# Row loads in two halves between the maxima transfers, and normalised tiles one per step, in a four-stage attention and mixture-of-experts kernel

## The chip, the cores and the metric

The kernel runs on one core of a Trainium2 chip. The metric is the device time of one execution in microseconds (us). Engines are named as in the profile: PE (TensorE matmul) and PEld (its weight loads), DVE (VectorE), ACT (ScalarE), POOL (GpSimd) and SP (SyncE, which here only issues transfers). SPq is SP's queue of instructions.

## What is computed

The input x is (4, 512, 256) in float32, the context has the same shape. Four stages follow each other, each adding to x: an attention without projections and with rotated queries and keys and a linear position bias (16 heads of 16), a top-1 expert layer, an attention with projections, and a top-k expert layer. The change touches the two attention stages alone.

```python
    x = x + _L0_xattn_ref(_layernorm(x, axis=-1), ctx_1024, ctx_1024, 16)
    x = x + _L0_ffn_ref(_layernorm(x, axis=-1), ...)
    x = x + _L1_xattn_ref(_layernorm(x, axis=-1), ctx_1024, ctx_1024, ...)
    x = x + _L1_ffn_ref(_layernorm(x, axis=-1), ...)
...
        scores = jnp.einsum('bqhd,bkhd->bhqk', q, k) * scale + bias[None]
        attn = jax.nn.softmax(scores, axis=-1)
        out = jnp.einsum('bhqk,bkhd->bqhd', attn, v)
```

## The kernel before, in words

One function, `attention`, makes both attention stages; `layer` is 0 or 1. The work is cut into 16 slots: slot s is batch b = s // 4 and group g = s % 4 of four heads. A slot takes four steps, one for each chunk of 128 keys, so step t belongs to slot t // 4 and a batch takes 16 steps. The program of each engine is written out as a loop over steps from -8 to 75.

For every half step PE makes a score tile with keys on the partitions (L596, `scores`), a second score tile with queries on the partitions for the row maxima of eight steps later (L581, `maxima_scores`, AHEAD = 8), and the weighted sum with the values (L615, `weigh`). The two score tiles share a ring of three units in PSUM: a new maxima tile takes the unit of the score tile whose exponentials ACT has just written (L719), and a new score tile the unit of the maxima tile that DVE has just reduced (L786). So PE waits for ACT one half step back.

The way of the maxima is: DVE reduces 8 tiles of slot s (L786), negates them (L792, L793), PE transposes them in step 4s-4 (L479, job "m"), ACT copies them to `max_t` (L655), and SP sends them into four more rows of `qa` (L364, `load_max(s)`, two transfers of 16 KB). PE needs them in step 4s, at the first score tile of slot s, which waits for `max_in`. m2, m6 and m10 stand below for `load_max` of slots 2, 6 and 10.

The rows of queries and keys of a batch come from two DRAM scratch tensors. `load(b, part)` fetches them: part 0 is groups 0 and 1 of the batch, part 1 is groups 2 and 3 (batch 0 is cut otherwise and is loaded ahead of the steps). Each part is four transfers of 384 KB (`rows_in_place`, L327): query rows and key rows, each for two partition halves; in layer 1 the key rows of batch 1 are loaded early, so that its parts have two transfers. Before the change both parts of a batch stand behind each other in SP's program, ahead of the maxima transfer of step 16b-12, which is m2, m6 and m10 for batches 1, 2 and 3. The maxima tiles need part 0 in step 16b-8 and part 1 in step 16b.

POOL rotates and splits the keys and queries of later batches and stores them in the scratch tensors: three transfers of 512 KB for the keys of a batch (L254), three of 256 KB for each pair i of query tiles (L259). Pair i is the half i % 2 of batch i // 2; there are eight.

For each pair ACT normalises two tiles of 128 x 256 (L687, `normed(i)`), two instructions behind each other at the start of step `q_at[i] - 3`; PE transposes them in step `q_at[i]` (L496), and ACT copies the result out (L664 in layer 0). In layer 0 `q_at` is 6 and 10 for pairs 4 and 5 and 22 and 26 for pairs 6 and 7, in layer 1 it is 2, 6, 18 and 22. In front of the exponentials the order is therefore: pair 4 in step 3, pair 5 in step 7 behind the copy of pair 4 in step 6, pair 6 in step 19, pair 7 in step 23 behind the copy of pair 6 in step 22. The first four pairs are normalised before the first exponential.

At the end of a slot (step 4s+4) ACT copies the slot's sums out of PSUM (L725, `a_out_sb`); two such copies in steady state lie one slot apart.

Of the kernel before, what the change touches and what calls it, by code (L numbers as in the profile page):

```python
# [6 lines left out]
ACT = mybir.ActivationFunctionType  # L7
# [8 lines left out]
B, T, D = 4, 512, 256  # L16
H, HD = 16, 16
# [6 lines left out]
NG = H // HG  # L24
# [119 lines left out]
def attention(nc, m, layer, dram):  # L144
# [8 lines left out]
    with ExitStack() as ctx:  # L153
# [77 lines left out]
        x = m.x  # L231
# [16 lines left out]
        def groups(b, part):  # L248
            cut = 1 if b == 0 else 2
            return (0, cut) if part == 0 else (cut, NG)  # L250
# [54 lines left out]
        with nc.Block() as block:  # L305

            @block.sync
            def _(sp):
# [26 lines left out]
                def load(b, part):  # L335

                    if part == 0:
                        if b == 0:
                            if layer == 0:
                                sp.wait_ge(k_first, 48)  # L340
                            sp.wait_ge(q_first, 96)
                        else:
                            if layer == 0:
                                sp.wait_ge(k_stored, 48 * b)
                            for j in range(2):
                                sp.wait_ge(q_stored[j], 48 * b)
                        if b >= 2:
                            sp.wait_ge(st_full, 8 * NG * (b - 1))
                    if layer == 1 and b >= 2:
                        load_keys(b, part)  # L350
                    for par in range(2):
                        rows_in_place(qa, q_scr, b, part, par).then_inc(loaded[part], 16)
                        if layer == 0:
                            rows_in_place(ka, k_scr, b, part, par).then_inc(loaded[part], 16)
# [40 lines left out]
                for t in steps:  # L395
                    for b in range(1, B):
                        if layer == 0 and b >= 2 and t == 16 * b - 38:
                            load_ctx(b)
                        for part in range(2):
                            if t == (2 if b == 1 else 16 * b - 14) + 2 * part:  # L400
                                load(b, part)
                    for job in ended.get((t, 1), []):
                        if job[0] == "m":
                            load_max(job[1])

            @block.gpsimd
            def _(pool):
# [238 lines left out]
            def _(act):  # L646
# [26 lines left out]
                            act.wait_ge(misc_full, index["a", b - 1, 1] + 1)  # L673
                        nc.scalar.copy(att_t[:, c], misc[:]).then_inc(misc_free, 1)

                def normed(i):

                    act.wait_ge(stats_done, (1 if i < 2 else 2) if layer == 0 else min(i // 2 + 1, 3))
                    if i >= 2:
                        act.wait_ge(misc_full, index[norm_kind, i - 2] + 1)  # L680
                    for j in range(2):
                        k = 2 * i + j
                        to, of = xn[:, i % 2, j], x[:, k]
                        if layer == 0:
                            to = to.rearrange("p (d e h) -> p h e d", e=2, d=HD)
                            of = of.rearrange("p (h e d) -> p h e d", e=2, d=HD)
                        nc.scalar.activation(to, of, ACT.Identity, bias=neg_mean[:, k:k + 1], scale=rstd[:, k:k + 1]).then_inc(xn_ready, 1)  # L687

                def values(n):

# [9 lines left out]
                        values(n)  # L700
                for job in first:
                    if job == (norm_kind, 0):
                        normed(0)
                        normed(1)
                    act_job(job)
                if layer == 1:
                    for n in range(4, 2 * B):
                        values(n)
                for t in steps:
                    for i in range(2, 2 * B):  # L710
                        if t == max(q_at[i] - 3, steps[0]):
                            normed(i)
                    for half in range(2):
                        n = 2 * t + half
                        if 0 <= t < STEPS:
# [1022 lines left out]
```

## Time and profile before

| what | value |
|---|---|
| device time, median of 3 runs (lowest, highest) | 1086.34 us (1085.20, 1089.04) |
| the profiled execution's own time | 1078.34 us |
| its span, first to last instruction | 1076.5 us |
| mean granted TensorE clock | 0.953 |
| PE busy | 944.4 us, 88% of the span |
| DVE, ACT, POOL busy | 605.6, 513.6, 300.5 us |
| layer 0's attention, about | first exponential at 75.2 us, last slot copied out near 265 us |
| layer 1's attention, about | first exponential at 565.2 us, end near 800 us |

The profiled execution lies 1.8 us above its span, and 8.0 us under the median of the timed runs. A PE that is busy 88% of the time still has gaps, and what they wait for is read from the timeline. Idle time of another engine costs only where PE waits for it.

### The profile page before, as it was taken

The numbers are of one execution on the slowest core, as the hardware profiler recorded it, in microseconds if no ns is written. First come the engines' busy times: TensorE is split into PE (matmuls) and PEld (weight loads), VectorE is DVE, ScalarE is ACT, GpSimd is POOL, SyncE is SP. The second block draws the span as 40 slices with busy tenths as digits, with TensorE's granted clock in tenths as the row PEclk, the third lists the DMA queues.
The fourth block names the chain that finished last, engine by engine and source line by source line (L and its number), as shares of the span: only waits on it lengthen the run. The fifth ranks groups of instructions, "written<-read, shape, count | busy, mean of one in ns | idle before, by whom it ended". The sixth has DMA issues, their size and how long they took to land. (4 is left out here: it accounts for less than half of the span.)

```text
span 1076.5 us, 17358 instructions
## 1 busy us (share of the span) xinstructions
PE 944.4 (88%) x6842; PEld 650.2 (60%) x6842; DVE 605.6 (56%) x1011; ACT 513.6 (48%) x777; POOL 300.5 (28%) x280
## 2 busy tenths in 40 slices
PE   0159999899798999999779999999979999999993
PEld 0023334343576999999653444444449999999993
DVE  7678979794432111110586766979314836655553
ACT  1027777678423322332326775767633035445550
POOL 5467843000001222221132122000000245554222
PEclk9999999899869999999997999999987999999997
DMA  9978372500439999996884061320006224555316
GB/s 159 234 206 200 94 195 58 96 4 4 153 134 373 325 338 345 339 345 220 186 202 91 33 119 62 73 51 4 4 2 236 79 59 133 141 169 146 98 21 175
DMA packets 52148, 158.96 MB, mean 148 GB/s; under 512 B 7792, under 2 KB 27888, under 8 KB 41392
## 3 DMA queue, kind: packets, MB, share of 16 engines
q1 hardware_dynamic: 35952, 121.96, 38.7%
q0 software_dynamic: 12912, 29.63, 11.3%
q10 hardware_dynamic: 3216, 6.43, 1.6%
q8 instruction: 47, 0.77, 0.3%
q14 instruction: 21, 0.17, 0.1%
HBM read 116.18 MB, written 40.76 MB: 146 GB/s over the span
## 5 line engine op out<-in xcount | busy, mean ns | idle before, releaser
L786 DVE TENSOR_REDUCE a_row_max<-ps_ring 128x2 f32<-128x1024 f32 x256 | 308.9, 1222 | 79.0 <-PE ps_ring L581 76.6
L719 ACT ACTIVATE a_probs<-ps_ring 128x1024 f32<-128x1024 f32 x256 | 260.7, 1022 | 102.1 <-PE ps_ring L596 100.2
L615 PE MATMUL ps_out<-a_probs,a_vaug 128*32 128x256 f32 x2048 | 166.7, 399 | 2.5 <-ACT a_out_sb L725 1.5
L581 PE MATMUL ps_ring<-a_ka,a_qa 52*128 52x512 f32 (+1 forms) x512 | 120.1, 473 | 54.4 <-DMA a_ka<-scratch_k_scr 44.2
L596 PE MATMUL ps_ring<-a_qa,a_ka 56*128 56x512 f32 (+1 forms) x512 | 131.7, 511 | 5.7 <-DMA a_qa<-a_max_t 3.7
L1056 ACT ACTIVATE e_hid<-ps_ring,e_wts 128x128 f32<-128x128 f32 x184 | 52.3, 368 | 120.2 <-PE ps_ring L1156 86.2
L596 PEld LDWEIGHTS ps_ring<-a_qa,a_ka 56*128 56x128 f32 (+1 forms) x512 | 49.1, 188 | 98.6 <-issue 67.3
L581 PEld LDWEIGHTS ps_ring<-a_ka,a_qa 52*128 52x128 f32 (+1 forms) x512 | 51.5, 199 | 86.9 <-issue 38.9
L1445 ACT ACTIVATE e_hr<-ps_ring 128x512 fp32r<-128x512 f32 x64 | 38.3, 598 | 118.9 <-PE ps_ring L1516 118.9
L1516 PE MATMUL ps_ring<-e_xt,e_wr 128*128 128x512 f32 x384 | 88.7, 390 | 0.4 <-DVE e_xt L1584 0.4
L615 PEld LDWEIGHTS ps_out<-a_probs,a_vaug 128*32 128x32 f32 x2048 | 41.1, 109 | 78.4 <-issue 72.2
L1156 PEld LDWEIGHTS ps_ring<-e_xst,e_wts 128*128 128x128 f32 x736 | 87.1, 195 | 1.9 <-issue 0.8
L1156 PE MATMUL ps_ring<-e_xst,e_wts 128*128 128x128 f32 x736 | 87.4, 278 | 0.6 <-DVE e_xst L1255 0.6
L1168 PE MATMUL ps_ring<-e_wts,e_hid 128*128 128x256 f32 x368 | 83.5, 380 | 0.3 <-ACT e_hid L1056 0.3
L1516 PEld LDWEIGHTS ps_ring<-e_xt,e_wr 128*128 128x128 f32 x384 | 71.6, 188 | 15.0 <-issue 0.6
L1604 DVE TENSOR_TENSOR e_hr<-e_hf,e_hr 128x512 fp32r<-128x512 f32 x64 | 44.4, 694 | 54.4 <-ACT e_hf L1448 54.4
L1168 PEld LDWEIGHTS ps_ring<-e_wts,e_hid 128*128 128x128 f32 x368 | 68.3, 191 | 8.8 <-ACT e_hid L1056 0.5
L1409 POOL DMA_INDIRECT scratch_acc<-e_ys,e_token x32 | 56.9, 1779 | 54.8 <-DVE e_ys L1598 50.9
L997 POOL DMA_INDIRECT scratch_ys<-e_ys,e_to_row x23 | 22.8, 993 | 121.6 <-DVE e_ys L1264 121.6
L1400 POOL DMA_INDIRECT e_xg<-scratch_xl,e_token x32 | 32.2, 1008 | 76.4 <-PE ps_ring L1500 47.9
L1264 DVE TENSOR_TENSOR e_ys<-ps_ring,e_wts 128x256 f32<-128x256 f32 x23 | 9.8, 425 | 74.9 <-PE ps_ring L1168 74.9
L1261 DVE TENSOR_TENSOR e_xst<-ps_misc,e_rms_t 128x256 f32<-128x256 f32 x22 | 9.3, 425 | 75.4 <-PE ps_misc L1137 75.4
(229 smaller groups left out, 1275.0 us busy)
## 6 DMA issues: line engine op xcount, KB each, us to landing
e_wts<-in_w SPq DMA_DIRECT2D x23, 1156.0 KB, 8.2
e_wts<-in_w SPq DMA_DIRECT2D x23, 1024.0 KB, 7.7
e_wf<-in_w SPq DMA_DIRECT2D x16, 1024.0 KB, 5.3
scratch_q_scr<-a_qst POOLq DMA_DIRECT2D x36, 256.0 KB, 3.2
a_qa<-scratch_q_scr SPq DMA_DIRECT2D x24, 384.0 KB, 10.2
a_ka<-scratch_k_scr SPq DMA_DIRECT2D x24, 384.0 KB, 12.2
scratch_k_scr<-a_kst POOLq DMA_DIRECT2D x9, 512.0 KB, 15.8
scratch_xl<-e_xn SPq DMA_DIRECT2D x8, 512.0 KB, 5.0
```

What stands on the lines that cost most here:

```text
L581: ins = pe.matmul(to[:, par], qa[rows, b % 2, g, p, qt * P:(qt + 1) * P], ka[rows, b % 2, g, p], start=True, stop=True)
L596: ins = pe.matmul(to[:, par], ka[rows, b % 2, g, p, kc * P:(kc + 1) * P], qa[rows, b % 2, g, p], start=True, stop=True)
L615: ins = pe.matmul(m.ps_out[VW * h:VW * (h + 1), cols], vaug[:, b % NV, kc, HG * g + h], probs[:, t % 3, h, cols], start=(kc == 0 and half ...
L719: nc.scalar.activation(probs[:, t % 3, 2 * half:2 * half + 2], unit("s", n), ACT.Exp, scale=HD ** -0.5).then_inc(exp_done, 1)
L786: dve.tensor_reduce(row_max[:, s % 3, qt, :, p], unit("m", n), AX.X, ALU.max).then_inc(mx_read, 1)
L1056: nc.scalar.activation(hid[:, k, fc], m.ps_st[:, 2 * k + half, q * P:(q + 1) * P], ACT.Silu, bias=wts[:, k, w1_cols + FC * D + fc:w1_cols ...
L1156: ins = pe.matmul(m.ps_st[:, 2 * k + half, q * P:(q + 1) * P], wts[:, k, c * F + fc * P:c * F + (fc + 1) * P], xst[:, k, c], start=(c == 0 ...
L1168: ins = pe.matmul(m.ps_max[:, k, 0:D], hid[:, k, fc], wts[:, k, w1_cols + fc * D:w1_cols + (fc + 1) * D], start=(fc == 0), stop=(fc == FC ...
L1409: pool.indirect_dma_start(dram["acc"], bass.IndirectOffsetOnAxis(token[:, e, b:b + 1], 0), ys[:, e % 2, b], None, compute_op=ALU.add).then ...
L1445: nc.scalar.activation(hr[:, 0, fc], m.ps_st[:, fc % 4], ACT.Gelu_apprx_tanh)
L1516: ins = pe.matmul(m.ps_st[:, fc % 4], wr[:, k, wp, c * F + fc * P:c * F + (fc + 1) * P], xt[:, xp, c], start=(c == 0 and (wp, xp) == (0, 0 ...
L1604: dve.tensor_tensor(hr[:, 1, fc], hf[:, fc % 4], hr[:, 0, fc].bitcast(F32), ALU.subtract).then_inc(h_split, 1)
```

## The change

In SP's program `load(b, part)` moves behind the maxima transfer of the same step, and its step becomes `16 * b - 15 + 4 * part` for every batch: part 0 in step 16b-15, behind the maxima transfer of step 16b-16, and part 1 in step 16b-11, behind that of step 16b-12. So one maxima transfer (m2, m6, m10) now stands between the two parts. Part 1 of batches 2 and 3 gets a wait of its own, for the first maxima tile of the batch before's group 2 (`mx_full`).

In ACT's program `normed(i)` becomes `normed(i, j)`, one tile each, in steps `q_at[i] - 4` and `q_at[i] - 3`. The first four pairs, which are normalised ahead of the exponentials, keep their order, and so does the loading of batch 0.

```diff
@@ load(b, part), SP @@
                         if b >= 2:
                             sp.wait_ge(st_full, 8 * NG * (b - 1))
+                    elif b >= 2:
+                        sp.wait_ge(mx_full, 8 * (NG * (b - 1) + groups(b, part)[0]) + 1)
@@ loop over steps, SP @@
-                        for part in range(2):
-                            if t == (2 if b == 1 else 16 * b - 14) + 2 * part:
-                                load(b, part)
                     for job in ended.get((t, 1), []):
                         if job[0] == "m":
                             load_max(job[1])
+                    for b in range(1, B):
+                        for part in range(2):
+                            if t == 16 * b - 15 + 4 * part:
+                                load(b, part)
@@ normed, ACT @@
-                def normed(i):
+                def normed(i, j):
...
-                    for j in range(2):
-                        k = 2 * i + j
...
-                        if t == max(q_at[i] - 3, steps[0]):
-                            normed(i)
+                        for j in range(2):
+                            if t == max(q_at[i] - 4 + j, steps[0]):
+                                normed(i, j)
```

SP's queue in layer 0 around the load of batch 3, before the change: the maxima transfer of slot 9 (L364), eight row loads (L327), then the maxima transfer of slot 10. Names in brackets are semaphores.

```order
L364 DMA a_qa<-a_max_t 4x2x512 [waits a0_st_full,a0_misc_free]
L364 DMA a_qa<-a_max_t 4x2x512
L327 DMA a_qa<-scratch_q_scr 48x2048 [waits a0_q_stored1,a0_st_full,a0_q_stored0,a0_k_stored]
L327 DMA a_ka<-scratch_k_scr 48x2048
L327 DMA a_qa<-scratch_q_scr 48x2048
L327 DMA a_ka<-scratch_k_scr 48x2048
L327 DMA a_qa<-scratch_q_scr 48x2048
L327 DMA a_ka<-scratch_k_scr 48x2048
L327 DMA a_qa<-scratch_q_scr 48x2048
L327 DMA a_ka<-scratch_k_scr 48x2048
L364 DMA a_qa<-a_max_t 4x2x512 [waits a0_st_full,a0_misc_free]
L364 DMA a_qa<-a_max_t 4x2x512
```

The same place of SP's queue after the change (line numbers are those of the changed file, where L366 is L364 of before):

```order
L327 DMA a_qa<-scratch_q_scr 48x2048 [waits a0_q_stored1,a0_st_full,a0_q_stored0,a0_k_stored]
L327 DMA a_ka<-scratch_k_scr 48x2048
L327 DMA a_qa<-scratch_q_scr 48x2048
L327 DMA a_ka<-scratch_k_scr 48x2048
L366 DMA a_qa<-a_max_t 4x2x512 [waits a0_st_full,a0_misc_free]
L366 DMA a_qa<-a_max_t 4x2x512
L327 DMA a_qa<-scratch_q_scr 48x2048 [waits a0_mx_full]
L327 DMA a_ka<-scratch_k_scr 48x2048
L327 DMA a_qa<-scratch_q_scr 48x2048
L327 DMA a_ka<-scratch_k_scr 48x2048
L366 DMA a_qa<-a_max_t 4x2x512 [waits a0_st_full,a0_misc_free]
L366 DMA a_qa<-a_max_t 4x2x512
```

The first maxima transfer in this piece is slot 10's: it had eight row loads ahead of it and now has four, and slot 11's, the last one here, now has four loads ahead of it where it had none.

ACT's queue in layer 0 in steps 4 to 8, before the change: the copy of slot 0's sums, the maxima copy of slot 2, four exponentials (steps 5 and 6), the copy of pair 4, both tiles of pair 5, four exponentials (steps 7 and 8) and the next copy of sums.

```order
L725 COPY a_out_sb<-ps_out 128x512
L655 CAST a_max_t<-ps_misc 8x512
L719 ACTIVATE a_probs<-ps_ring 128x1024 x4
L664 COPY a_qx<-ps_misc 128x512
L687 ACTIVATE a_xn<-x_res,a_neg_mean,a_rstd 128x8x2x16 x2
L719 ACTIVATE a_probs<-ps_ring 128x1024 x4
```

The same piece after the change:

```order
L729 COPY a_out_sb<-ps_out 128x512 [waits a0_pv_done]
L658 CAST a_max_t<-ps_misc 8x512 [waits a0_max_in0,a0_misc_full]
L723 ACTIVATE a_probs<-ps_ring 128x1024 [waits a0_pv_done,a0_st_full] x2
L689 ACTIVATE a_xn<-x_res,a_neg_mean,a_rstd 128x8x2x16 [waits a0_misc_full,a0_stats_done]
L723 ACTIVATE a_probs<-ps_ring 128x1024 [waits a0_pv_done,a0_st_full] x2
L667 COPY a_qx<-ps_misc 128x512 [waits a0_q_ready,a0_misc_full]
L689 ACTIVATE a_xn<-x_res,a_neg_mean,a_rstd 128x8x2x16 [waits a0_misc_full,a0_stats_done]
L723 ACTIVATE a_probs<-ps_ring 128x1024 [waits a0_pv_done,a0_st_full] x4
```

One of the two tiles went from step 7 to the start of step 6, ahead of that step's two exponentials; the copy of pair 4 and the other tile stayed.

## Rows read from the trace of the kernel before

**Rows 1.** The page: busy time of PE over the whole span.

```profile
PE 944.4 (88%) x6842; PEld 650.2 (60%) x6842; DVE 605.6 (56%) x1011; ACT 513.6 (48%) x777; POOL 300.5 (28%) x280
```

**Rows 2.** Waits: who waited for L364, whole span (us, times); PE's wait, 75 to 265 us.

```profile
  PE ps_ring L596: 3.7, 2
...
PE ps_ring L581 <- ACT a_probs L719: 3.6, 4, 1.2
```

**Rows 3.** Timeline of SP's queue in layer 0: start, length, line, transfer, count.

```profile
91.92 1.35 SPq L364 DMA_DIRECT2D a_qa<-a_max_t  x2
...
143.61 1.35 SPq L364 DMA_DIRECT2D a_qa<-a_max_t  x2
...
183.96 0.32 SPq L327 DMA_DIRECT2D a_qa<-scratch_q_scr  x1
...
194.06 1.35 SPq L364 DMA_DIRECT2D a_qa<-a_max_t  x2
```

**Rows 4.** One transfer at a time: issue and time from issue to landing, us.

```profile
L327 SPq DMA_DIRECT2D a_ka<-scratch_k_scr x1: 422/422/422, 185.3 to 185.3; - x1
DMA to landing us min/median/max: 10.5/10.5/10.5
...
L327 SPq DMA_DIRECT2D a_ka<-scratch_k_scr x1: 423/423/423, 187.3 to 187.3; - x1
DMA to landing us min/median/max: 17.6/17.6/17.6
...
L254 POOL DMA_DIRECT2D scratch_k_scr<-a_kst x2: 731/731/731, 90.2 to 91.0; - x2
DMA to landing us min/median/max: 13.0/13.7/14.5
```

**Rows 5.** Timeline of PE, layer 0; in brackets idle time ahead and its releaser.

```profile
99.97 0.50 PE L581 MATMUL ps_ring<-a_ka,a_qa 52*128 52x512 f32 x2 [1.16 <-ACT a_probs L719]
100.39 0.64 PE L615 MATMUL ps_out<-a_probs,a_vaug 128*32 128x256 f32 x8
...
102.05 0.50 PE L596 MATMUL ps_ring<-a_qa,a_ka 56*128 56x512 f32 x2 [0.43 <-DMA a_qa<-a_max_t]
...
103.28 0.49 PE L596 MATMUL ps_ring<-a_qa,a_ka 56*128 56x512 f32 x2
...
138.14 0.50 PE L581 MATMUL ps_ring<-a_ka,a_qa 52*128 52x512 f32 x2 [0.65 <-ACT a_probs L719]
...
151.67 0.50 PE L581 MATMUL ps_ring<-a_ka,a_qa 52*128 52x512 f32 x2 [1.17 <-ACT a_probs L719]
152.09 1.07 PE L615 MATMUL ps_out<-a_probs,a_vaug 128*32 128x256 f32 x8
...
155.97 0.50 PE L596 MATMUL ps_ring<-a_qa,a_ka 56*128 56x512 f32 x2
...
205.12 0.80 PE L596 MATMUL ps_ring<-a_qa,a_ka 56*128 56x512 f32 x2 [3.23 <-DMA a_qa<-a_max_t]
```

**Rows 6.** Stretch 152 to 154 us: busy time of each engine, PEclk, DMA share, GB/s.

```profile
152.00:154.00 2.00, 2.00 (x14) 0.91 (x12) 1.64 (x3) 0.52 (x1) 1.86 (x4) 0.54 0.33 80
```

**Rows 7.** Timeline of ACT, layer 0: the copies at the ends of three slots.

```profile
181.35 0.59 ACT L725 COPY a_out_sb<-ps_out 128x512 f32<-128x512 f32 x1
...
192.99 0.58 ACT L725 COPY a_out_sb<-ps_out 128x512 f32<-128x512 f32 x1
...
221.60 0.59 ACT L725 COPY a_out_sb<-ps_out 128x512 f32<-128x512 f32 x1
```

**Rows 8.** Timeline of ACT in step 19 of layer 0: pair 6, then two exponentials.

```profile
135.83 1.41 ACT L687 ACTIVATE a_xn<-x_res,a_neg_mean,a_rstd 128x256 f32<-128x256 f32 x2
137.04 1.95 ACT L719 ACTIVATE a_probs<-ps_ring 128x1024 f32<-128x1024 f32 x2
```

**Rows 9.** Waits of PE in layer 1, 560 to 660 us: us, times, longest.

```profile
PE ps_ring L581 <- ACT a_probs L719: 0.6, 2, 0.4
```

**Rows 10.** Timeline of DVE and POOL, layer 0: the negations beside POOL's work.

```profile
101.77 0.24 DVE L792 TENSOR_SCALAR a_neg_max<-a_row_max 128x16 fp32r<-128x16 f32 x1
...
126.17 1.29 DVE L792 TENSOR_SCALAR a_neg_max<-a_row_max 128x16 fp32r<-128x16 f32 x1
...
126.14 1.28 POOL L282 TENSOR_TENSOR a_kf<-a_kf 128x512 f32<-128x512 f32 x1
```

More of the change, by code:

```diff
@@ L680, in normed @@
                         act.wait_ge(misc_full, index[norm_kind, i - 2] + 1)
-                    for j in range(2):
-                        k = 2 * i + j
[L683 to L687, printed above, removed]
+                    k = 2 * i + j
+                    to, of = xn[:, i % 2, j], x[:, k]
+                    if layer == 0:
+                        to = to.rearrange("p (d e h) -> p h e d", e=2, d=HD)
+                        of = of.rearrange("p (h e d) -> p h e d", e=2, d=HD)
+                    nc.scalar.activation(to, of, ACT.Identity, bias=neg_mean[:, k:k + 1], scale=rstd[:, k:k + 1]).then_inc(xn_ready, 1)
                 def values(n):
@@ L702, in _ @@
                     if job == (norm_kind, 0):
-                        normed(0)
-                        normed(1)
+                        for i in range(2):
+                            for j in range(2):
+                                normed(i, j)
                     act_job(job)
@@ L710, in _ @@
                     for i in range(2, 2 * B):
-                        if t == max(q_at[i] - 3, steps[0]):
-                            normed(i)
+                        for j in range(2):
+                            if t == max(q_at[i] - 4 + j, steps[0]):
+                                normed(i, j)
                     for half in range(2):
```

## Prediction

> **What bounds the kernel now.** I began with the page: PE is busy for 944.4 us, 88% of the span [rows 1], so a change that takes no work from PE can only win what PE loses in gaps, and what PE loses by running at the lower clock behind a gap. The next view was who waits for the two things that the change touches. For the maxima transfers (L364) PE's matmuls wait 3.7 us in two places, and for the exponentials in layer 0 they wait 3.6 us in four places [rows 2]. Then the timelines of PE, SP and ACT, to see what is ahead of each wait.
>
> The two waits for maxima are the first score tile of slot 2, at 102.05 us with 0.43 us of idle time, and that of slot 10, at 205.12 us with 3.23 us [rows 5]. Slot 10's transfers were issued at 194.06 us, 10 us after the row loads of batch 3 began at 183.96 us [rows 3]. The last row load, issued at 187.3 us, landed 17.6 us later, at 204.9 us; the fourth of the eight, issued at 185.3 us, landed after 10.5 us, at 195.8 us [rows 4]. PE goes on 0.2 us after the last of the eight has landed. The maxima are small and are served behind 3 MB of rows: I read it as a queue in order, and the landing times grow evenly along it.
>
> What it costs is more than the wait. Slots end at 181.35 and 192.99 us, 11.64 us apart; the next two take 28.61 us together, to 221.60 us [rows 7], against 23.28 us. So batch 3's stall costs **5.3 us**: 3.2 us of wait, and 2.1 us in which the matmuls behind it take 0.80 us in place of 0.50 us [rows 5].
>
> At batch 2 there is little wait for maxima, but a low clock: from 152 to 154 us the granted clock is 0.54 [rows 6], nearly the lower level of 1.2 GHz. From the weighted sum at 152.09 us to the score tile at 155.97 us it is 3.88 us; the same row of work at batch 1 takes 2.89 us, from 100.39 to 103.28 us, of which 0.43 us is the wait [rows 5]. So 3.88 - 2.46 = **1.4 us** is lost. What PE did before the clock fell was to stand still for 1.17 us at 151.67 us [rows 5], for ACT.
>
> That is the second kind of gap. ACT normalises two tiles in 137.04 - 135.83 = 1.21 us ahead of the exponentials of a step [rows 8], and PE's next maxima tile waits for the first of these: 0.65 us at 138.14 us, and 1.16 and 1.17 us where the copy of the pair before also stands ahead (99.97 and 151.67 us) [rows 5]. The fourth of the four, pair 4's, is what is left of 3.6 us, about 0.6 us [rows 2].
>
> **The change, part by part.**
>
> *Loads in halves.* No transfer is added or dropped. m2, m6 and m10 have four loads ahead of them in place of eight. By the landing times of batch 3 the fourth has landed at 195.8 us [rows 4], so m10, issued at 194.06 us [rows 3], should be in place near 196 to 197 us, 5 us before PE asks at about 201.9 us. At batches 1 and 2 POOL's key stores share the engines, but half of 20 us of loads still leaves m2 and m6, issued at 91.92 and 143.61 us [rows 3], several us in hand. So the waits go: 0.4 us at batch 1, and 5.3 us at batch 3, its low clock included. For batch 2 the bounds are 0 (the clock falls all the same) and 1.4 us; I take 1.4 us, since the gap that stands ahead of the fall shrinks as well, next paragraph.
>
> What is queued behind: SP waits for nothing new in fact. The new wait of part 1 (batches 2 and 3) is for a maxima tile of step 16b-16, and the transfer ahead of it in SP's queue belongs to step 16b-12, which is later. Behind part 1 stands the maxima transfer of the next slot (m3, m7, m11). It comes a slot, 11.6 us, after part 1, and four loads take 195.8 - 184.0 = 11.8 us, so it lands about 1 us late at most, and PE wants it four steps after its issue. Part 1's rows are wanted in step 16b and are issued in step 16b-12 or so, three slots, 35 us, ahead. Cost nothing; without that cover a late part 1 would stop PE for as long as it is late.
>
> *Tiles one per step.* The same instructions, each 0.605 us of ACT. A step without other work has hidden 1.21 - 0.65 = 0.56 us of the pair, so a single tile costs it 0.05 us. For pairs 4 and 6: 0.65 becomes 2 x 0.05, saved 0.55 us each. For pairs 5 and 7 the step behind the copy goes from 1.165 us to 1.165 - 0.605 = 0.56 us, and the step before pays 0.05 us: saved 0.5 us each. Together **2.1 us**. Bounds: 0 if the step that takes the tile over has no room, 3.6 us if all four gaps close. I take the middle by the slack read at 138.14 us.
>
> *Layer 1.* No wait of PE for maxima is left for it: the two of layer 0 make up 0.43 + 3.23 of the 3.7 us in the whole span [rows 2, 5]. Its waits for exponentials around the pairs are 0.6 us in two places [rows 9]; I take 0.2 us, bounds 0 and 0.6 us. The loads' halves win nothing there.
>
> *DVE beside POOL.* One row speaks for a loss. The negation at 126.17 us took 1.29 us beside a POOL tensor operation from 126.14 us that took 1.28 us; at 101.77 us it took 0.24 us [rows 10]. The order on POOL and DVE is unchanged, but the slots with a copy of queries get half a microsecond shorter, so a negation can start half a microsecond earlier against POOL's work. From the row: at worst one POOL operation of 1.3 us more is waited for, in each of two slots. The slot of 101.77 us is one of the two, and there the negation was hardly held, so I take the row that is nearest: cost 0, bounds 0 and 2.6 us. The Trainium skill (SBUF — State Buffer, section "SBUF: two separate sides") says that DVE and GpSimd share a pair of ports as a lock, which one holds for a whole instruction while the other is fully blocked. By that rule, the trace agrees (1.29 against 0.24 us), and it is the one rule there that speaks for a loss; by it in full the sum below would be 2.6 us less.
>
> **Sum.** 0.4 + 1.4 + 5.3 + 2.1 + 0.2 = **9.4 us** of 1078.34 us, the profiled execution's own time, so 1068.9 us for an execution like it. The median of the runs shown lies 8.0 us above that execution; I carry the gain over unchanged: 1086.3 - 9.4 = **1076.9 us**. Low end of the gain: 0.4 + 0 + 5.3 + 0 + 0 - 2.6 = 3.1 us; high end: 0.4 + 1.4 + 5.3 + 3.6 + 0.6 = 11.3 us.
>
> **Rivals.** A measurement of this kernel tells no change from one of about 0.3%, 3.3 us.
>
> *The halves of the tiles win nothing (faster still).* PE is fully busy in the steps that take the tile over, so each tile moves its delay along. For it: ACT's slack there is only half a microsecond. Against: the two kinds of gap, 0.65 and 1.16 us, differ by just about the copy, as a slack used up once would have it. Gain 9.4 - 2.1 = 7.3 us, 1079.0 us.
>
> *The maxima are not served in the queue's order (no change).* Part 1 is issued right behind m10 and could get ahead of it, as m10 fills only eight partitions. Then m10 lands with the last of the rows as before. For it: one cannot see the maxima's own landing in the trace. Against: in all places PE goes on just when the rows ahead have landed, with nothing behind them to compare. Gain only 2.1 + 0.2 = 2.3 us, 1084.0 us.
>
> *The key stores hold the maxima (slower).* At batches 1 and 2 POOL stores 1.5 MB of keys while the loads run. If m2's completion had to wait for them, it would come when the third store lands, issued at 91.0 us and 14.5 us on its way, at 105.4 us [rows 4], while PE would now ask for it at 101.6 - 1.1 = 100.5 us: a wait of 4.9 us, and the like at batch 2, 9.8 us together, against 5.3 + 2.3 = 7.6 us won elsewhere. That is 2.2 us slower, 1088.5 us, and more with a fall of the clock behind each wait. It decides from 3.8 us per wait on. Against it: before the change PE went on at 102.05 us [rows 5], 3.4 us before that store had landed. The Trainium skill (DMA: Bandwidth & Descriptors, section "Queues, rings and completion order") has a rule of this kind: a transfer's semaphore increment lands only after every earlier write of its DMA engine, across queues. By that rule the stores could hold m2; the trace bears it out only weakly, as the 3.4 us show. The same section says that each engine consumes one queue's descriptors in order and takes turns between queues, with which the 0.2 us at slot 10 agrees.
>
> **How the numbers follow.** Chances: the forecast 0.80, tiles win nothing 0.07, maxima not in order 0.08, key stores 0.05. Faster 0.87, within 0.3% 0.08, slower 0.05. The predicted time is the forecast's, 1076.9 us. Its own range is 1086.3 - 11.3 to 1086.3 - 3.1, 1075.0 to 1083.2 us; the timed runs of before spread by about 2 us to either side, and the stretches of low clock need not fall in the timed runs as they did in this profile, so I widen to 1071.5 to 1083.5 us, which leaves out the no-change and the slower case.
>
> **What would show it.** In layer 0: no PE wait for `a_max_t` at slots 2, 6 and 10; all slots of batch 2 and later without a query pair at 11.6 us, that of slot 9 among them (16.6 us before); granted clock 1.0 from 150 to 260 us; PE's waits for exponentials down from 3.6 to about 1.4 us; eight single tiles of 0.6 to 0.7 us on ACT; loads in two groups 12 us apart, m3, m7 and m11 without a wait. In layer 1 the same length within 0.5 us. I am wrong if PE still waits at slot 10, if m7 or m11 becomes a wait, or if slots without a stall grow by a DVE negation of over 1 us.

## The result, and the profile after

In the first comparison, four executions of each kernel, the changed kernel took **1068.88 us** (1067.97 to 1072.19) and the kernel before 1087.69 us (1085.20 to 1089.82). The ratio is **0.983**, 95% interval 0.980 to 0.987: by the medians 18.8 us faster, where 9.4 us was forecast. 1068.88 us lies under the low end of the range. Of every kernel below, executions more than 1.5% longer than its shortest are left out of the ratios (one of e1, three each of e5 and e16, two of e10), but not out of the medians and ranges. The profiled execution of the changed kernel took 1068.09 us against 1078.34 us before, 10.25 us less.

Its page, busy times over the whole span, answers to [rows 1]: PE's work is the same number of instructions, 4.8 us shorter.

```profile
PE 939.6 (88%) x6842; PEld 645.7 (61%) x6842; DVE 605.4 (57%) x1011; ACT 514.1 (48%) x777; POOL 300.1 (28%) x280
```

PE's waits in layer 0's attention, 60 to 260 us (us, times, longest), answer to [rows 2]: no row for `a_max_t` is left, and the wait for the exponentials fell from 3.6 us in four places to 1.2 us in two.

```profile
PE ps_ring L584 <- ACT a_probs L723: 1.2, 2, 0.6
```

SP's queue around the load of batch 3, and the landing of each half's last row load, answer to [rows 3, 4]. Columns as there.

```profile
182.16 0.42 SPq L327 DMA_DIRECT2D a_ka<-scratch_k_scr  x1
190.98 1.35 SPq L366 DMA_DIRECT2D a_qa<-a_max_t  x2
192.37 0.44 SPq L327 DMA_DIRECT2D a_qa<-scratch_q_scr  x1
...
202.64 1.35 SPq L366 DMA_DIRECT2D a_qa<-a_max_t  x2
```

```profile
L327 SPq DMA_DIRECT2D a_ka<-scratch_k_scr x1: 422/422/422, 182.2 to 182.2; - x1
...
DMA to landing us min/median/max: 11.0/11.0/11.0
...
L327 SPq DMA_DIRECT2D a_ka<-scratch_k_scr x2: 422/422/422, 192.9 to 193.8; - x2
...
DMA to landing us min/median/max: 6.9/8.9/10.8
```

Part 0's last load landed at 182.2 + 11.0 = 193.2 us, 2.2 us behind the issue of m10 and 5.5 us ahead of the score tile that needs it, at 198.75 us, which has no idle time ahead of it. Part 1's last row load lands only at 193.8 + 10.8 = 204.6 us, so m10 was in place before the rows issued behind it, 5.8 us at the least. PE, the timeline at the two places where pairs 5 and 7 stand, and at slots 2 and 10 (it answers to [rows 5]):

```profile
99.74 0.49 PE L584 MATMUL ps_ring<-a_ka,a_qa 52*128 52x512 f32 x2 [0.59 <-ACT a_probs L723]
...
101.32 0.50 PE L599 MATMUL ps_ring<-a_qa,a_ka 56*128 56x512 f32 x2
...
149.89 0.50 PE L584 MATMUL ps_ring<-a_ka,a_qa 52*128 52x512 f32 x2 [0.58 <-ACT a_probs L723]
...
198.75 0.50 PE L599 MATMUL ps_ring<-a_qa,a_ka 56*128 56x512 f32 x2
```

The window of [rows 6] now has PEclk 1.00, and the copies of sums at the ends of slots 8, 9 and 10 (ACT's timeline, answering to [rows 7]) are 11.66 and 11.65 us apart, where batch 3's stall was:

```profile
152.00:154.00 2.00, 2.00 (x22) 0.69 (x20) 1.97 (x4) 1.77 (x2) 1.86 (x3) 1.00 0.88 131
```

```profile
189.90 0.59 ACT L729 COPY a_out_sb<-ps_out 128x512 f32<-128x512 f32 x1
...
201.56 0.59 ACT L729 COPY a_out_sb<-ps_out 128x512 f32<-128x512 f32 x1
...
213.21 0.59 ACT L729 COPY a_out_sb<-ps_out 128x512 f32<-128x512 f32 x1
```

Pair 6 is now two tiles, one in each of two steps (ACT's timeline; [rows 8] shows the pair in one row):

```profile
132.49 0.82 ACT L689 ACTIVATE a_xn<-x_res,a_neg_mean,a_rstd 128x256 f32<-128x256 f32 x1
...
135.10 0.82 ACT L689 ACTIVATE a_xn<-x_res,a_neg_mean,a_rstd 128x256 f32<-128x256 f32 x1
```

**The slots of layer 0.** The distance between two copies of sums is a slot. This table is the ruler for all runs below; the slots not in it agree within 0.1 us in the full kernels (slot 0 aside, see the end) but for slot 2 of e2, 12.93 against 12.33 us; in e5 and e16 slots 2 and 6 are up to 0.8 us longer. The traces of e5 and e16 are of long executions, 298.05 us and 299.27 us, where the medians are 296.31 and 295.81 us. The first two rows are the profiles of before and after, and `e...` are the runs of the next section.

```
us                        slot 1  slot 4  slot 5  slot 9  slot 10
before                     13.97   13.78   14.91   16.64   11.97
after                      13.05   13.17   13.06   11.66   11.65
e3  before, again          14.47   13.76   13.80   15.41   12.29
e4  changed, again         13.28   13.19   13.04   11.63   11.65
e1  loads in halves alone  13.51   13.78   13.52   11.64   11.64
e2  tiles alone            16.10   13.21   13.37   16.55   11.92
e8  before, m10 on POOL    16.28   13.78   14.59   16.36   12.21
e5  stage of before        13.74   13.75   17.36   18.09   12.40
e16 stage of before, again 16.07   13.77   17.00   17.59   12.40
```

### The profile page after: what moved, and what is told of

Its sections match the earlier page's. It is cut to its first block and busy times, and to the rows that moved or that the text cites. A ratio compares the mean times of both kernels' runs of the same rounds, so it can differ in the third digit from the quotient of the medians.

```text
span 1066.3 us, 17370 instructions
## 1 busy us (share of the span) xinstructions
PE 939.6 (88%) x6842; PEld 645.7 (61%) x6842; DVE 605.4 (57%) x1011; ACT 514.1 (48%) x777; POOL 300.1 (28%) x280
## 6 DMA issues: line engine op xcount, KB each, us to landing
scratch_k_scr<-a_kst POOLq DMA_DIRECT2D x9, 512.0 KB, 12.5
```

## The experiments

**The two kernels again, and each part alone** (e1 to e4, one chip, shared with 29 executions of the kernel before, median 1085.57 us, 1079.24 to 1093.26). e3 and e4 have no edit. e1 is the SP part of the diff alone, e2 the ACT part alone:

```diff
@@ e1: loop over steps, SP; ACT as before @@
+                    for b in range(1, B):
+                        for part in range(2):
+                            if t == 16 * b - 15 + 4 * part:
+                                load(b, part)
@@ e2: loop over steps, ACT; SP as before @@
-                        if t == max(q_at[i] - 3, steps[0]):
-                            normed(i)
+                        for j in range(2):
+                            if t == max(q_at[i] - 4 + j, steps[0]):
+                                normed(i, j)
```

> The loads' half of the change alone: row loads in two halves behind maxima transfers, both normalised tiles of a pair in one step as before. The two profiles at hand give the whole change 10.2 us, the timed runs about 18 us. Theory A (the timed executions of the kernel before lose more at the maxima waits and at the low clock behind them than its one profiled execution did): this part alone gives 14 to 17 us of the timed gain. Theory B (the tiles' half of the change is worth more in timed runs than in the profile): it gives 7 us or less. Theory C (the runs shown were drawn from different stages of luck, and the change is worth the 10 us of the profiles): 6 to 8 us. In its trace PE waits for no maxima transfer and still waits about 3.6 us for exponentials in layer 0.

> The tiles' half alone: normalised tiles one per step, row loads as before. By the prediction's sum 2.1 us of gain by the tiles, and up to 1.4 us more if the fall of the clock at batch 2 came from the 1.17 us gap. Theory A: 1 to 4 us. Theory B: 8 to 12 us. Theory C: 2 to 3 us. In its trace the maxima waits at slots 2 and 10 stay or grow, since PE asks earlier, and the waits for exponentials fall from 3.6 to about 1.4 us.

> The kernel before, unchanged, for a second trace and for how far one execution of it lies from another. Theory A: its trace is 5 to 10 us longer than the first one, and the difference lies in layer 0 at slots 2, 6 and 10, with more low clock there. Theory C: the difference lies in other stages or there is none. Timed, no difference: within 0.3%.

> The changed kernel, unchanged, beside the other three on the same chip. Theory A: 15 to 19 us faster than before, and equal to the sum of the two halves within 3 us. Theory C: 9 to 12 us faster. Trace within 2 us of the first one of the changed kernel.

Measured, 12 executions each of e1 to e3 and 6 of e4: **e1 1077.12 us, ratio 0.993** (0.990 to 0.996); **e2 1086.01 us, ratio 1.000** (0.997 to 1.002); **e3 1082.61 us, 0.998** (0.994 to 1.001); **e4 1072.79 us, 0.989** (0.985 to 0.993). By the ratios the loads alone gain 7.5 us, the tiles alone 0.3 us and both together 11.9 us; the intervals are too wide (4.1 to 10.9 us for e1, 7.2 to 16.7 us for e4) to say from the times that the parts don't add up. The traces say it: behind slot 0, layer 0's attention is 5.8 to 7.2 us shorter in e1 than in the two traces of before, 0.6 to 2.0 us longer in e2, and 7.1 to 8.5 us shorter in the changed kernel. The waits of e2, PE in layer 0, show where the tiles' gain went:

```profile
PE ps_ring L596 <- DMA a_qa<-a_max_t: 6.1, 3, 3.8
...
PE ps_ring L581 <- ACT a_probs L720: 1.2, 2, 0.6
```

```profile
103.88 0.50 PE L596 MATMUL ps_ring<-a_qa,a_ka 56*128 56x512 f32 x2 [2.09 <-DMA a_qa<-a_max_t]
```

The exponentials' wait fell by 2.4 us, as in the changed kernel, and the maxima's grew by as much, 3.7 to 6.1 us: PE comes earlier to a transfer that lands when the rows have landed. At slot 2 the wait grew by more than the tiles can give, from 0.43 to 2.09 us, so part of it is this execution's own. In e1 the other half shows: no wait for maxima, and the one for exponentials as it was.

```profile
PE ps_ring L584 <- ACT a_probs L722: 3.7, 4, 1.2
```

e1 also tells against a reason of mine. The gap of 1.17 us that stood ahead of the low clock in batch 2 [rows 5] is still there in e1, but the granted clock stays 1.0. First e1's row of PE, then the window in which [rows 6] have 0.54, in two pieces:

```profile
150.93 0.51 PE L584 MATMUL ps_ring<-a_ka,a_qa 52*128 52x512 f32 x2 [1.17 <-ACT a_probs L722]
```

```profile
152.00:153.00 1.00, 1.00 (x8) 0.65 (x8) 0.93 (x2) 0.00 (x0) 0.94 (x2) 1.00 1.02 139
153.00:154.00 1.00, 1.00 (x14) 0.34 (x10) 0.96 (x4) 0.94 (x1) 0.92 (x2) 1.00 0.96 147
```

And e3, the kernel before itself, holds 1.0 there too:

```profile
144.00:158.00 14.00, 12.63 (x112) 5.15 (x109) 11.02 (x13) 10.95 (x14) 6.54 (x8) 1.00 0.70 188
```

So the 1.4 us of batch 2 belonged to some executions and not to every one.

**The stages apart.** e5 and e6 keep layer 0's attention of the kernel before and of the changed one and leave the three later stages out; e7 keeps the three later stages of the kernel before and leaves the first out. e9 is e5 with the loads in halves (on another chip than e5 to e7).

```diff
@@ the end of the program, e5, e6, e9; e7 has stages[1:] behind a load of x @@
-        for stage in stages:
-            stage()
+        stages[0]()
```

> Layer 0's attention of the kernel before, alone: the other three stages are left out, and x is stored behind it. From the traces at hand: 273.9 to 274.4 us to the last copy of sums, so about 285 us in all. Theory A (the timed executions lose more at the maxima waits than the traces show): its runs spread by 5 us or more, and lie 12 us or more above those of the changed layer alone. Theory C (the stage is worth what the traces show, and the rest of the timed difference comes from the clock in the other stages): spread under 3 us, and 7 to 9 us above the changed one.

> Layer 0's attention with the change, alone: the other three stages are left out. Theory A: 12 us or more below the same stage of before. Theory C: 7 to 9 us below it, as in the traces (191.7 to 193.2 us against 199.1 to 199.5 us from the first exponential on).

> The three stages behind the first attention, alone (of the kernel before; the first attention is left out, so x goes straight into the top-1 experts and the routing differs): how far executions of the rest lie apart. Theory C: spread of 8 to 12 us between its runs, going with the mean granted clock, and most of the spread of the whole kernel. Theory A: under 5 us.

> Layer 0's attention alone (the other three stages left out), with the loads in halves and both tiles of a pair in one step. The same stage took 296.3 us before and 284.7 us with the whole change. If the loads carry the stage's gain: 285.5 to 288 us, runs within 3 us of each other, no wait for maxima; the tiles are then worth 1 to 3 us behind the halves. If the tiles matter more through the clock: 289 us or more.

Measured: e5 296.31 us (291.59 to 299.87, 6 executions), **e6 284.67 us** (283.49 to 285.52, 5), e9 286.76 us (285.71 to 288.07, 5), e7 802.27 us (799.39 to 804.90, 4). The difference e5 - e6 is 11.6 us by the medians of all executions; by the three of e5 that count in the ratio it is 294.20 - 284.67 = 9.5 us. By the same measure the halves alone are worth 294.20 - 286.76 = 7.4 us, where the prediction's terms for them are 7.1 us. The tiles are worth 286.76 - 284.67 = **2.1 us** behind the halves, the forecast's number. More telling is the spread: 8.3 us among six executions of the old stage, 2.0 us among five of the new one. e5's PE timeline at slots 6 and 10: the first was no wait in [rows 5], the second is longer, and the matmuls take 0.8 us behind both:

```profile
158.20 0.80 PE L596 MATMUL ps_ring<-a_qa,a_ka 56*128 56x512 f32 x2 [2.05 <-DMA a_qa<-a_max_t]
...
212.59 0.79 PE L596 MATMUL ps_ring<-a_qa,a_ka 56*128 56x512 f32 x2 [4.67 <-DMA a_qa<-a_max_t]
```

**The maxima on another queue** (e8: the kernel before, but slot 10's two maxima transfers are issued by POOL, with a semaphore of their own; all eight row loads stay ahead of them in time, on SP's queue).

```diff
@@ loop over steps, POOL @@
+                    if layer == 0 and t == 36:
+                        s = 10
...
+                            pool.dma_start(qa[rows, s // NG % 2, s % NG].bitcast(F32),
```

> The kernel before, whole bursts of eight row loads, but the two maxima transfers of slot 10 in layer 0 issued by POOL's queue and counted by a semaphore of their own. If the order within SP's queue is what holds them, as predicted: no wait of PE for maxima at slot 10, slots 9 and 10 at 11.7 us each, layer 0 shorter by 4 to 5 us. If the 16 DMA engines are simply full (a rival not in the prediction): PE waits at slot 10 as before, 3 us or more. The waits at slots 2 and 6 stay.

One execution, 1073.61 us. POOL issued the maxima at 199.04 us, 7.2 us behind the last row load; PE went on only at 209.54 us. POOL's timeline, then SP's last row load and its landing, then PE's timeline:

```profile
199.04 1.18 POOL L464 DMA_DIRECT2D a_qa<-a_max_t  x2 [2.12 <-ACT a_max_t L672]
```

```profile
L336 SPq DMA_DIRECT2D a_ka<-scratch_k_scr x1: 422/422/422, 191.8 to 191.8; - x1
...
DMA to landing us min/median/max: 17.5/17.5/17.5
```

```profile
209.54 0.79 PE L613 MATMUL ps_ring<-a_qa,a_ka 56*128 56x512 f32 x2 [2.95 <-DMA a_qa<-a_max_t]
```

The last rows landed at 191.8 + 17.5 = 209.3 us, and PE went on 0.2 us later, just as in [rows 4, 5]. So place in SP's queue is not what holds the maxima: on a queue of its own a 16 KB transfer is still complete only when 3 MB of earlier rows are. Slots 9 and 10 take 28.57 us together, before 28.61 us.

The DMA view shows when the packets themselves moved (queue, number of packets, MB, share of 16 engines; q1 is SP's queue, q0 POOL's). First e8 from 199.0 to 206.8 us, then from 206.8 to 209.0 us:

```profile
q1 hardware_dynamic: 218, 1.35, 101.2%
```

```profile
q1 hardware_dynamic: 31, 0.12, 33.1%
q0 software_dynamic: 64, 0.03, 10.7%
```

POOL's two transfers were issued at 199.04 us, and for 7.8 us not one of their 64 packets moved, while 218 of the rows' did. The same shows between other transfers, and in both directions. Before the change, POOL's key stores, issued from 89.5 us on behind row loads, moved nothing up to 97.0 us; in the changed kernel, SP's m2, issued at 92.12 us behind the key stores, moved nothing from 92.1 to 94.0 us:

```profile
q1 hardware_dynamic: 218, 1.35, 103.7%
```

```profile
q0 software_dynamic: 210, 0.76, 101.9%
```

With no rows ahead, POOL's queue is not slow: of its stores issued from 104.4 us on, before the change, the first packets moved before 105.5 us.

The Trainium skill (DMA: Bandwidth & Descriptors, section "Queues, rings and completion order") says that a transfer's semaphore increment lands only after every earlier write of its DMA engine, across queues. e8's times agree with that, 209.54 against 209.3 us, but do not test it, since the packets themselves moved late. The turns between queues of which the same section speaks don't show in these rows, 218 packets to none.

**Both halves behind the maxima** (e10, the new stage alone, the other three left out) and **the tiles a step earlier** (e11 in the stage alone, e12 in the full changed kernel):

```diff
@@ e10, SP @@
-                            if t == 16 * b - 15 + 4 * part:
+                            if t == 16 * b - 11:
@@ e11, e12, ACT @@
-                            if t == max(q_at[i] - 4 + j, steps[0]):
+                            if t == max(q_at[i] - 5 + j, steps[0]):
```

> Layer 0's attention alone, with the tiles one per step, but both parts of a batch behind each other again, one slot later than before: behind the maxima transfers of slots 2, 6 and 10 and ahead of those of slots 3, 7 and 11. If the length of the whole burst (20.6 us from the first issue to the last landing) against a slot is what stops PE: the waits for maxima move to slots 3, 7 and 11, 2 to 4 us each, and the stage takes 293 to 298 us. If the place of the burst was the matter: no such wait, and 284 to 287 us. A small wait for the rows of part 0 is possible in either case, since they are wanted four steps after their issue.

> Layer 0's attention alone, changed stage, with the two tiles of a pair another step earlier (steps q_at - 5 and q_at - 4), so that no tile stands behind the copy of the pair before. If the gaps of 0.6 us left in steps 7 and 23 come from copy and tile together: they go, the two slots with a pair and a copy take 12.5 us in place of 13.06, the stage 1 us less (283.5 us). If ACT's slack is used up in those steps anyway: no change.

> The whole changed kernel with the tiles another step earlier, as in e11, in both attention layers. If the gaps go: 1 us under the changed kernel, that is 1070 to 1073 us and 11 to 15 us under before; not to be told from it by timing alone, so the slots in the trace decide. A loss in layer 1 would show as a slot longer than 15.2 or 21.7 us.

e10 took **306.25 us** (302.94 to 309.74), about 21 us more than e6, and by neither theory: m3, m7 and m11 were no wait, but PE now waited for the rows of part 0 themselves. Its waits and the first place:

```profile
PE ps_ring L584 <- DMA a_ka<-scratch_k_scr: 15.2, 3, 5.4
```

```profile
109.94 0.79 PE L584 MATMUL ps_ring<-a_ka,a_qa 52*128 52x512 f32 x2 [5.35 <-DMA a_ka<-scratch_k_scr]
```

The eight loads were issued from 96.48 us on, PE wanted part 0 8.1 us later and had it after 13.5 us. So part 0 can't be issued three steps ahead of its need; the changed kernel's seven are enough. The experiment did not test what I meant it for, whether a burst of eight holds the next maxima.

e11 took 283.48 us (282.24 to 285.63), 1.2 us less than e6 with the ranges overlapping, on another chip; e12 **1070.89 us, ratio 0.990** (0.986 to 0.993), no better than the changed kernel. The 0.6 us gaps do not close, they move to the step with the copy of sums (e12, PE's timeline), and in layer 1 slots 3 and 4 grew by 0.46 and 0.49 us:

```profile
93.83 0.49 PE L584 MATMUL ps_ring<-a_ka,a_qa 52*128 52x512 f32 x2 [0.58 <-ACT a_probs L723]
...
143.88 0.51 PE L584 MATMUL ps_ring<-a_ka,a_qa 52*128 52x512 f32 x2 [0.61 <-ACT a_probs L723]
```

**Where the rest of 18.8 us is** (e13 to e16, another chip, shared with 11 executions of the kernel before, median 1082.45 us, 1077.95 to 1093.95). e13 is the changed kernel without an edit, e14 is e7 again, e15 the same cut of the changed kernel (layer 0's attention left out), e16 is e5 again.

> The changed kernel a third time, with more runs of both. If the true gain is what the stages show (7 to 9.5 us in layer 0, 0.6 us in layer 1): 8 to 12 us, ratio 0.989 to 0.9925. If the first comparison (18.8 us, four runs each) showed something real beyond the stages: 15 us or more.

> The three stages behind the first attention, alone, of the kernel before, a second time: 799 to 805 us as the first time.

> The same three stages of the changed kernel (layer 0's attention left out): from the traces of layer 1, 0.6 us less than before. If the timed gain beyond the stage of layer 0 is real and comes from the other stages: 3 us or more less. If not: within 2 us.

> Layer 0's attention of before, alone, a second time (other three stages left out). If its ordinary executions lose more at the maxima than the first trace did: median of the undisturbed runs 294 us or more. If they lose the same: 292 to 294 us, that is 7.5 to 9.5 us above the changed stage. In the trace: waits at slots 2, 6 and 10 of 3.5 to 7 us in all.

Measured: **e13 1075.34 us, ratio 0.988** (0.982 to 0.994); e14 810.61 us (805.25 to 811.71); e15 806.06 us (801.93 to 808.21), with ratios to the kernel before of 0.7475 (0.7443 to 0.7507) and 0.7434 (0.7399 to 0.7469); e16 295.81 us (290.94 to 299.77). e16's trace, slots 1, 5 and 9, and each window's PEclk (third number from the end) at 0.84 to 0.86:

```profile
92.89:108.96 16.07, 14.11 (x109) 5.50 (x108) 11.32 (x13) 10.78 (x15) 9.73 (x13) 0.85 0.87 218
...
147.49:164.49 17.00, 14.13 (x110) 5.45 (x109) 11.34 (x13) 10.75 (x14) 8.92 (x11) 0.84 0.74 196
...
200.69:218.28 17.59, 13.43 (x106) 5.11 (x105) 11.27 (x13) 9.13 (x10) 0.72 (x1) 0.86 0.66 106
```

The stages of the whole kernels, from the traces (us). An attention runs from its first exponential to its last copy of sums, and the expert layers are what lies behind each; "behind slot 0" is layer 0's attention from the first copy of sums on. The last column is the whole execution:

```
                        layer 0  behind slot 0  first experts  layer 1  last experts  execution
before                   199.13         183.53         290.87   225.03        286.25    1078.34
e3  before, again        199.51         182.15         290.51   222.86        291.34    1080.41
e8  before, m10 on POOL  202.66         185.52         289.96   221.09        281.74    1073.61
e2  tiles alone          199.09         184.16         291.43   224.21        290.53    1083.42
e1  loads alone          191.86         176.37         291.93   224.76        284.79    1070.20
after                    191.68         175.04         294.95   222.07        283.22    1068.09
e4  changed, again       193.20         175.09         291.87   222.84        287.52    1071.24
e13 changed, third       189.94         174.93         297.48   223.98        288.22    1076.94
```

The expert layers are untouched by the change, and the last one alone takes 281.74 to 291.34 us. Its windows before, in e3 and after (PEclk 0.93, 0.92, 0.94), and the first expert layer's in e13:

```profile
790.25:1076.50 286.25, 260.94 (x1740) 240.93 (x1740) 157.72 (x304) 106.29 (x157) 98.51 (x67) 0.93 0.42 118
```

```profile
787.26:1078.60 291.34, 264.48 (x1740) 244.19 (x1740) 157.73 (x304) 106.41 (x157) 98.54 (x67) 0.92 0.41 116
```

```profile
783.08:1066.30 283.22, 257.52 (x1740) 237.40 (x1740) 157.67 (x304) 106.39 (x157) 98.49 (x67) 0.94 0.42 120
```

```profile
265.42:562.90 297.48, 271.18 (x1668) 236.17 (x1668) 86.69 (x266) 90.23 (x255) 61.64 (x63) 0.91 0.81 268
```

This answers what e3 was run for. Its execution is 2.1 us longer than the first profile of the same kernel, and layer 0 is not the reason: behind slot 0 it is 1.4 us shorter, while the last expert layer is 5.1 us longer. e8 has the longest layer 0 of the eight, and yet the shortest execution of the four that keep the eight row loads together (before, e3, e8, e2). e14 missed its forecast of 799 to 805 us: the same kernel took 802.27 us on e7's chip and 810.61 us on e14's.

By their ratios (1 less the ratio, times the time before) the three comparisons of the same two kernels gave 18.2, 11.9 and 12.9 us. The first is of four executions each, with an interval of 14.6 to 21.6 us; the later ones, of 6 against 29 and 6 against 11, agree, with 7.2 to 16.7 and 6.7 to 19.0 us. I take the change's worth to be near 12.5 us, and the rest of the first figure to be its draw. That is argued and not shown, as the timed executions have no traces; the untouched stages above are wide enough for it.

## Why the prediction was right or wrong

**The waits for maxima: right.** None is left at slots 2, 6 and 10, in any trace of a kernel with halves. The reading of the cause was half right: the maxima are complete when the rows issued ahead of them are, but e8 shows that it is not the order of one queue: on another queue their packets don't move either until the rows are almost through.

**The rival that the maxima are not served in order: refuted.** With part 1 issued behind m10, PE went on at 198.75 us without a wait, and part 1's rows landed only at 204.6 us.

**Batch 3, 5.3 us: right for that execution.** Slots 9 and 10 went from 28.61 to 23.31 us, 5.3 us; from e3's 27.70 us it would be 4.4 us. **Batch 1:** 13.97 to 13.05 us is 0.92, the forecast's 0.4 + 0.5. **Batch 2, 1.4 + 0.5 us:** 14.91 to 13.06 us is 1.85. The number came out, the reason did not: I tied the low clock to the gap of 1.17 us, which e1 keeps without a fall, and e3 has no fall with the old order. That the number came out is luck: measured from e3's 13.80 us it is 0.74 us. What makes the clock fall there in one execution and not in another stays open.

**The tiles, 2.1 us: right.** 2.1 us in the stages alone (e9, e6, on two chips); from e1's trace to the changed kernel's 0.46, 0.61 and 0.46 us at slots 1, 4 and 5, where 0.5, 0.55 and 0.5 were forecast. Pair 4's share lies in slot 0, which varies by more than that. The rows of single tiles, for which I wrote 0.6 to 0.7 us, are longer: each shows 0.82 us by itself, as two behind each other overlap and took 1.41 us together [rows 8]; what a tile costs PE was still as forecast. What I didn't say is that the gain depends on the other half: alone none shows (ratio 1.000, 0.997 to 1.002), since the maxima take it back (e2).

**Layer 1:** 0.2 us forecast; slot 3 went from 12.16 to 11.68 us and slot 4 by 0.1 us, 0.6 us together, the upper bound. The whole stage was 3.0 us shorter in the profile after, against the 0.5 us that I had given it; 2.5 us of that lie in its slot 0 (20.97 and 18.50 us), which takes 18.72 us in e3, so it can be short with the old order too.

**DVE beside POOL, 0: right.** The hold moved. At slot 2 it is now the second negation that takes 0.63 us, and it ends at 102.37 us beside a POOL tensor operation that runs from 101.61 to 102.34 us; before, the two took 0.24 us [rows 10] and 0.18 us; the slot of 12.33 us stayed at 12.33 us. DVE's timeline of the changed kernel:

```profile
101.53 0.17 DVE L796 TENSOR_SCALAR a_neg_max<-a_row_max 128x16 fp32r<-128x16 f32 x1
101.74 0.63 DVE L797 SCALAR_TENSOR_TENSOR a_neg_max<-a_row_max,a_neg_max 128x16 fp32r<-128x16 f32 x1
```

**The rival with the key stores: refuted.** It took the store's landing, 14.5 us [rows 4], to be fixed. With part 0 landed first, the three stores, issued from 88.6 to 90.1 us, land in 4.2 to 5.3 us, so by 95.4 us, 6 us before PE asks at 101.32 us. m2 does stand behind the stores, as the packets from 92.1 to 94.0 us show; it costs nothing because they are done in time. Landing times of a queue of transfers are no property of the transfer.

**The sum: right for the stages that it was read from, wrong for the two medians.** Behind slot 0 the terms for layer 0 are 0.4 + 1.4 + 5.3 + 1.55 = 8.65 us, and the two profiles differ there by 183.53 - 175.04 = 8.5 us; with layer 1's 0.6 us it is 9.1 us. That the whole profiles differ by 10.25 us, so near 9.4 us, is in part luck: the first expert layer was 4.1 us longer after, the last 3.0 us shorter and layer 1's slot 0 2.5 us shorter. The change does not touch the two expert layers, and e3 has that slot 0 short without it.

**The step that failed:** "The median of the runs shown lies 8.0 us above that execution; I carry the gain over unchanged", with "about 2 us to either side" for how far executions lie apart. It puts the difference between two draws of four executions at next to nothing. The runs showed it to be as large as the gain: executions of the kernel before lie from 1079.24 to 1093.26 us on one chip, those of the changed one from 1062.11 to 1076.94 us on another, and the untouched last expert layer alone takes 281.74 to 291.34 us in the traces. The forecast of 9.4 us lies inside the intervals of both repeated comparisons (7.2 to 16.7 and 6.7 to 19.0 us) and outside the first one's (14.6 to 21.6 us).

A second, smaller part is that the stall is not of one size, so the terms 0.4, 1.4 and 5.3 should have had a range of their own. Behind slot 0 the old order took 7.1 us (e3), 8.5 (before) and 10.5 (e8) longer than the changed kernel's 175.04 us; in the stage alone, in its long executions, it was 13.4 (e5) and 15.6 us (e16), with a low clock in e16's slots 1, 5 and 9. The wait at slot 10 was 2.97 us (e3), 3.23 (before) and 4.67 (e5). I had expected (theory A) that the longer executions of the whole kernel are those that lose more here. The traces don't show that: e3 is longer than the first profile and loses less, e8 is shorter and loses more. e1's 7.5 us also lies by theory C's 6 to 8 us and not by theory A's 14 to 17 us.

**What stays open.** The stage alone gained 9.5 us (e5 against e6, on one chip; 9.7 us with e16's three that count), against 7.1 to 8.5 us behind slot 0 in the whole kernels' traces, and layer 1 0.6 us. That is 7.7 to 10.3 us of some 12.5, with intervals of the timed gain that hold both. Where the first comparison's further 6 us were is not known. e14 and e15 differ by 4.6 us in the rest, but their intervals overlap, and their profiled spans are 803.1 and 803.4 us; whether the later stages gain by more than layer 1's 0.6 us isn't settled. Nor is what holds a transfer on another queue: the packets show that it starts late, in three places, and not why.

## What to carry to other kernels

A small transfer that the compute waits for should be issued where no large load is on its way, whichever queue either is on; half the load ahead of it and half behind it cost nothing here, as both halves were still early enough. Where two waits stand in a row, the first one's gain is real only when the second is gone, so try the parts together as well as alone. A stall read from one profile gives one draw of its size, and the medians of four executions each can differ by as much as the gain: compare the stages that the change does not touch across several traces of one kernel, and take the range from them.

## What the hardware showed that was not expected

- A transfer of 16 KB on POOL's queue, issued 7.2 us behind the last row load on SP's, was in place with the last rows: 209.54 against 209.3 us (e8). None of its 64 packets moved in the 7.8 us behind its issue, while 218 of the rows' did.
- The same gap of 1.17 us in the same place was followed by a granted clock of 0.54 in one execution (the lower level, 1.2 GHz, for most of two microseconds) and of 1.00, 2.4 GHz, in another (e1).
- One kernel's executions lie between 1079.24 and 1093.26 us on one chip in one session, with mean granted clocks of 0.956 and 0.945; the stage of before alone spreads by 8.9 us over twelve executions, the changed one by 2.0 us over five.
- Slot 0 of layer 0 takes 15.0 to 18.1 us in the traces of the two kernels (both ends are the changed one's, e13 and e4; before 15.6, e3 17.4). All that the change does in it is to move one tile of pair 4 by a step, which was forecast at 0.55 us.
